# Four-layer graph network kernel: layer 3's bias, relu and residual on other engines, the layer-1 softmax finished in columns, and new piece orders

## The reference

```
x = layernorm(x + (hyperconv2(layernorm(relu(hyperconv1(x)))) + x))                # layer 0
# layer 1, per graph of 64 nodes
w = mask * rowsum(q * (adj @ (k * mask))) / sqrt(256)
x = layernorm(x + softmax(w over the graph's 64 nodes)[:, None] * (x @ Wv))
x = layernorm(x + multi_head_attention(x, scores * 2 adj))                          # layer 2, 8 heads
# layer 3
gate = sigmoid(deg * Wd + bd);  xg = x * gate
QK = sigmoid(xg @ Wqk.T + bqk); S = (QK @ QK.T) / 16 * adj
out = relu((S / (rowsum(S) + 1e-6)) @ xg @ Wl.T + bl + xg @ Wr.T)
x = layernorm(x + out)
```

## Time and profile before

| | |
|---|---|
| three runs | 1066.08, 1060.98, 1060.03 us; median 1060.98 |
| span of the profiled execution, first to last instruction | 1059.4 us; no own total beside the three runs is listed for it |
| median less span | 1.6 us |
| PE busy | 956.5 us, 90% |
| DVE busy | 886.8 us, 84% |
| POOL busy | 777.8 us, 73% |
| ACT busy | 710.6 us, 67% |
| chain that ended last | DVE 33%, PE 25%, issue 14%, ACT 13%, POOL 12% |
| granted PE clock | mean 0.972; 1.00 in all middle stretches |
| DMA queue of the kernel's transfers | 22.2% of 16 engines |

### The profile page before, as it was taken

One profiled execution on the slowest core, in us unless ns is written; L12 is line 12 of the kernel. 1 busy time (PEld: TensorE's weight loads), 2 busy tenths in 40 slices (PEclk: granted clock), 3 DMA queues, 4 the chain that ended last, 5 costly groups with the idle time before them and its releaser, 6 DMA issues.

```text
span 1059.4 us, 32426 instructions
## 1 busy us (share of the span) xinstructions
PE 956.5 (90%) x11164; PEld 808.6 (76%) x11164; DVE 886.8 (84%) x2564; ACT 710.6 (67%) x1516; POOL 777.8 (73%) x1163
## 2 busy tenths in 40 slices
PE   3368999999999999999999999999999999999873
PEld 2256788888888888888888888888888888887752
DVE  4346888898989989989998998989999998989862
ACT  2335677777776677777776677777776777776642
POOL 3155778778877788788877788788877887786542
PEclk9589999999999999999999999999999999999986
DMA  7110221222222122222222112222212112211110
GB/s 206 31 33 9 64 61 53 69 68 59 67 57 61 51 53 57 67 57 67 67 55 62 50 52 60 67 57 67 67 53 62 50 51 62 67 45 42 46 39 20
DMA packets 110231, 61.80 MB, mean 58 GB/s; under 512 B 57072, under 2 KB 105840, under 8 KB 110192
## 3 DMA queue, kind: packets, MB, share of 16 engines
q1 hardware_dynamic: 110192, 61.30, 22.2%
HBM read 35.83 MB, written 8.39 MB: 42 GB/s over the span
## 4 chain that ended last, share of the span: by engine, by line
DVE 33%; PE 25%; issue 14%; ACT 13%; POOL 12%; DMA 1%; DVEq 1%; SPq 0%; POOLq 0%; ACTq 0%
PE bank L460 7%; PE bank L462 6%; PE bank L461 6%; DVE preG L1176 4%; DVE rFl L999 3%; ACT x L735 3%; POOL y0l L1200 3%; ACT r L762 2%; DVE late L1171 2%; PE bank L485 2%; DVE ql L900 2%; PE bank L634 2%; DVE stG L947 2%; DVE PTl L894 2%; DVE xgFl L894 2%
## 5 line engine op out<-in xcount | busy, mean ns | idle before, releaser
L1102 DVE TENSOR_TENSOR late<-bank,acD 128x512 f32<-128x512 f32 x64 | 44.2, 690 | 51.3 <-PE bank L634 50.9
L735 ACT ACTIVATE x<-preB,nbB,rsB 128x256 f32<-128x256 f32 x64 | 35.0, 593 | 68.0 <-POOL nbB L1212 68.0
L460 PE MATMUL bank<-z1h,W 128*128 128x256 f16 x256 | 71.0, 277 | 3.1 <-DVE z1l L894 3.0
L461 PE MATMUL bank<-z1l,W 128*128 128x256 f16 x256 | 70.9, 277 | 0.0
L460 PE MATMUL bank<-W,rFh 128*128 128x256 f16 x256 | 70.8, 277 | 0.0
L462 PE MATMUL bank<-z1h,W 128*128 128x256 f16 x256 | 70.8, 277 | 0.0
L462 PE MATMUL bank<-W,rFl 128*128 128x256 f16 x256 | 70.5, 275 | 0.0
L461 PE MATMUL bank<-W,rFh 128*128 128x256 f16 x256 | 70.5, 275 | 0.0
L1287 POOL TENSOR_TENSOR late<-late,Smx 128x512 f32<-128x512 f32 x64 | 67.0, 1046 | 0.0
L735 ACT ACTIVATE late<-preG,nbG,rsG 128x256 f32<-128x256 f32 x64 | 34.9, 593 | 47.0 <-POOL nbG L1212 46.9
L1200 POOL TENSOR_TENSOR y0l<-y,y0h 128x512 f16<-128x512 f32 x32 | 55.5, 1736 | 1.5 <-ACT y0h L719 1.5
(11 more groups left out here) (284 smaller groups left out, 4625.1 us busy)
## 6 DMA issues: line engine op xcount, KB each, us to landing
Vbd<-vst SPq DMA_DIRECT2D x128, 66.0 KB, 2.1
xin<-x SPq DMA_DIRECT2D x32, 256.0 KB, 2.7
...
Kbd<-kst SPq DMA_DIRECT2D x128, 64.0 KB, 2.0
...
```

The source lines that it names most:

```text
L460: pe.matmul(o, sh, mh, start=start, stop=False, skip_group_check=True)
L461: pe.matmul(o, sh, ml, start=False, stop=False, skip_group_check=True)
L735: m = act.activation(dst[:, t], pre[k][:, t], ACT.Identity, bias=nb[k][:, t:t + 1], scale=rs[k][:, t:t + 1])
L1102: dve.tensor_tensor(Sm[:, t], (bD0, bD1)[t][:].rearrange("p (h k) -> p h k", h=HEADS), acD[:, at.par, t:t + 1].broadcast_to([P, HEADS, NOD ...
```

## The change

Three things change.

1. Layer 3's tail. Before: ACT casts Wr's product out of PSUM into `o2` (scaled), POOL adds the bias `blb` to it, DVE makes `o3` and then `preG` = max(`o3`, 0) + `x3` in one instruction. After: DVE reads Wr's product from PSUM, scales it and adds the bias in one instruction; DVE makes `o3` as before; ACT takes the relu of `o3` into a new tile `o3r`; POOL adds `x3` and writes `preG`.
2. The layer-1 softmax. Before, the differences `wrm` (2 partitions) go through exp, sum, reciprocal and product on 2 partitions, and the product is turned back. After, `wrm` is turned back at once, exp is taken on 128 partitions x 2 columns from PSUM, the sums come from a float32 matmul with a block matrix of ones (`same`), and reciprocal and product are on 128 x 2. DVE loses two pieces, PE gains one, and 1/16 moves into `wpad`.
3. All four order lists are new. In full, PE's:

```diff
-ORDER_PE = [4, 2, 5, 4, 1, 3, 0, 5, 4, 3, 2, 0, 1, 5, 0, 2, 4, 0, 0, 5, 3, 1, 5, 3, 5, 2, 1, 3, 2, 1, 0, 3, 4, 0]
+ORDER_PE = [4, 2, 3, 1, 5, 3, 0, 4, 2, 5, 0, 4, 2, 1, 5, 0, 3, 2, 3, 0, 0, 1, 5, 4, 5, 1, 3, 5, 2, 3, 0, 0, 1, 2, 4]
...
             def stream2(at):
...
-                pe.wait_ge(ev("w_probs"), at.n()).then_inc(ev("pe_held"), 1)
-                pe.transpose(bC[:, 0:TILES], wpr[:].rearrange("t b k -> t (b k)"), ident[0:TILES, 0:TILES]
-                             ).then_inc(ev("p_turned"), 1)
+                pe.wait_ge(ev("w_shifted"), at.n()).then_inc(ev("pe_held"), 1)
+                pe.transpose(bC[:, D:D + TILES], wrm[:].rearrange("t b k -> t (b k)"), ident[0:TILES, 0:TILES]
+                             ).then_inc(ev("w_back"), 1)
+                yield
+                pe.wait_ge(ev("w_exp"), at.n())
+                pe.matmul(bC[:, D + TILES:D + 2 * TILES], same[:], wex[:], start=True, stop=True
+                          ).then_inc(ev("w_sum"), 1)
                 yield
...
-                act.wait_ge(ev("w_shifted"), at.n())
-                act.activation(wex[:], wrm[:], ACT.Exp, scale=SOFT1).then_inc(ev("w_exp"), 1)
+                act.wait_ge(ev("w_back"), at.n())
+                act.activation(wex[:], bC[:, D:D + TILES], ACT.Exp).then_inc(ev("w_exp"), 1)
...
-                act.wait_ge(ev("o2_raw"), at.n())
-                if at.earlier(1):
-                    act.wait_ge(ev("mixed"), at.n(-1))
-                cast(o2[:].rearrange("p t k -> p (t k)"), bG[:], 1.0 / WS).then_inc(ev("o2"), 1)
+                act.wait_ge(ev("mixed"), at.n())
+                if at.earlier(1):
+                    act.wait_ge(ev("preG"), at.n(-1))
+                act.activation(o3r[:], o3[:], ACT.Relu).then_inc(ev("o3_relu"), 1)
...
-                dve.wait_ge(ev("w_exp"), at.n())
-                dve.tensor_reduce(wsm[:], wex[:], AX.X, ALU.add).then_inc(ev("c_softmax"), 1)
-                yield
-                dve.wait_ge(ev("c_softmax"), at.chain(3, 2))
-                dve.reciprocal(wrc[:], wsm[:]).then_inc(ev("c_softmax"), 1)
-                yield
-                dve.wait_ge(ev("c_softmax"), at.chain(3, 3))
-                dve.tensor_tensor(wpr[:], wex[:], wrc[:].rearrange("t (b o) -> t b o", o=1).broadcast_to(
-                    [TILES, 2, NODES]), ALU.mult).then_inc(ev("w_probs"), 1)
-                yield
-                dve.wait_ge(ev("p_turned"), at.n())
-                dve.tensor_scalar(pcol[:], bC[:, 0:TILES], 1.0 / WS, None, ALU.mult).then_inc(ev("p_col"), 1)
+                dve.wait_ge(ev("w_sum"), at.n())
+                dve.reciprocal(wrc[:], bC[:, D + TILES:D + 2 * TILES]).then_inc(ev("c_softmax"), 1)
+                yield
+                dve.wait_ge(ev("c_softmax"), at.chain(2, 2))
+                dve.scalar_tensor_tensor(out=pcol[:], in0=wex[:], scalar=1.0 / WS, in1=wrc[:], op0=ALU.mult,
+                                         op1=ALU.mult).then_inc(ev("p_col"), 1)
...
+                dve.wait_ge(ev("o2_raw"), at.n())
+                dve.scalar_tensor_tensor(out=o2[:], in0=bG[:].rearrange("p (t k) -> p t k", t=TILES), scalar=1.0 / WS,
+                                         in1=blb[:].rearrange("p (o d) -> p o d", o=1).broadcast_to([P, TILES, D]),
+                                         op0=ALU.mult, op1=ALU.add).then_inc(ev("o2"), 1)
+                yield
...
-                dve.wait_ge(ev("mixed"), at.n())
-                dve.scalar_tensor_tensor(out=pre["G"][:].rearrange("p t k -> p (t k)"),
-                                         in0=o3[:].rearrange("p t k -> p (t k)"), scalar=0.0,
-                                         in1=x3[:, at.par].rearrange("p t k -> p (t k)"), op0=ALU.max, op1=ALU.add
-                                         ).then_inc(ev("preG"), 1)
-                yield
...
-                pool.wait_ge(ev("o2"), at.n())
-                bias_tm(o2[:], o2[:], blb).then_inc(ev("o2_biased"), 1)
+                pool.wait_ge(ev("o3_relu"), at.n())
+                if at.earlier(1):
+                    pool.wait_ge(ev("xG"), at.n(-1))
+                pool.tensor_tensor(pre["G"][:], o3r[:], x3[:, at.par], ALU.add).then_inc(ev("preG"), 1)
```

More of the change, by code:

```diff
@@ L184, in build @@
         wpad = sb("wpad", [P, P])
+        same = sb("same", [P, P])
+        wmx = sb("wmx", [TILES, 2])
         wrm = sb("wrm", [TILES, 2, NODES])
-        wmx = sb("wmx", [TILES, 2])
-        wex = sb("wex", [TILES, 2, NODES])
-        wsm = sb("wsm", [TILES, 2])
-        wrc = sb("wrc", [TILES, 2])
-        wpr = sb("wpr", [TILES, 2, NODES])
+        wex = sb("wex", [P, TILES])
+        wrc = sb("wrc", [P, TILES])
         pcol = sb("pcol", [P, TILES])
@@ L218, in build @@
         gt = sb("gt", [P, TILES, D])
+        o3r = sb("o3r", [P, TILES, D])
         g2 = sb("g2", [P, TILES, D])
@@ L906, in _ @@
             dve.memset(onesf[:], 1.0).then_inc(ev("const"), 1)
-            for buf in (atA, aC, atG, wpad):
+            for buf in (atA, aC, atG, wpad, same):
                 dve.memset(buf[:], 0.0).then_inc(ev("const"), 1)
-            dve.wait_ge(ev("const"), 6)
+            dve.wait_ge(ev("const"), 7)
+            for b in range(2):
+                dve.memset(same[64 * b:64 * b + 64, 64 * b:64 * b + 64], 1.0).then_inc(ev("const"), 1)
+            dve.wait_ge(ev("const"), 9)
             dve.wait_ge(ev("ident"), 3).then_inc(ev("cleared"), 1)
@@ L1045, in stream1 @@
                 dve.wait_ge(ev(f"C_in{at.par}"), at.dma(4))
-                dve.tensor_tensor(wpad[:, 0:TILES], wraw[:], mcol[:, at.par], ALU.mult).then_inc(ev("w_masked"), 1)
+                dve.scalar_tensor_tensor(out=wpad[:, 0:TILES], in0=wraw[:], scalar=SOFT1, in1=mcol[:, at.par],
+                                         op0=ALU.mult, op1=ALU.mult).then_inc(ev("w_masked"), 1)
                 yield
@@ L1054, in stream2 @@
                 yield
-                dve.wait_ge(ev("c_softmax"), at.chain(3, 1))
+                dve.wait_ge(ev("c_softmax"), at.chain(2, 1))
                 dve.tensor_tensor(wrm[:], wv, wmx[:].rearrange("t (b o) -> t b o", o=1).broadcast_to(
```

8 lines of the change are left out of this document (4 added, 4 removed).

## The result

The changed kernel takes 1074.31 us (median of 4 runs, 1073.73 to 1074.63) beside 1062.18 for the kernel before (4 runs on the same chip): a ratio of 1.0116, 95% interval 1.0092 to 1.014. It is slower by a little over 1%. I had forecast 1046.5.

The account below looks back on a forecast made before the run. PE's own work plus its waits, mostly on DVE, was taken as the bound: 27.9 + 0.7 + 0.1 + 0.45 + 0.15 = 29.3 us a step. With -15.7 and +1.3 in the drain, 1046.5 us; range 1028 to 1074.

Parts of the forecast that it names:

- Times 27 filled steps: Filled pipeline: 0.58 us less a step than 29.88, over 27 steps, gives -15.7 us.
- wrm's chain: PE ready to turn `wrm`, but DVE makes `Dbg`, `cx`, `Dd`, `wrm` first: 0.7 us a step lost, dearest wait.
- y3l: PE's s3 wants `y3l` at 10.3, after the end of `y3`, a cast and `y3l` itself: 0.1 us lost.
- row sums: PE waits while POOL's `rsq` sums and DVE's `rFl` alternate: 0.3 us lost plus 0.15 for waits, in place of 0.54.
- xg turned: PE's turn of `xg` waits for relu, POOL's added `preG` and `xg` in sequence: 0.15 us lost.
- DVE 25.0: DVE's work a step, 2.2 us less: 25.0 us in place of 27.2.
- Gaps that close: PE's old waits at `wpad`, `xgFl`, `PTl` and `y0l` were to vanish.
- Tail of the last group: In the drain, relu 0.61 and POOL's addition 1.28 with handoffs replace `preG` 0.69: +1.3 us.
- first rival: `HBl` split by POOL's `x2b` in the loop, delaying PE's product: 30.3 us a step, 1073.7 us; chance 0.2.
- Other things that would have shown it wrong: PE waiting on ACT or on the K blocks' DMAs would be wrong in kind; `preG` on POOL expected near 1.28.
- Gain turns into other waits: `pcol` and `Ql` held by POOL on DVE, PE late at layer 3's row sum: 29.8 a step, 1060 us; chance 0.21.
- slack is worth more: Only the `wrm` wait is real on PE: 28.5 us a step, 1025 us; chance 0.15.

Follow-up runs that it names:

- e1: Changed kernel with the old order lists, fitted to the new pieces, in its first six steps; 1067.24 us.
- e10: The kernel of e7 with the old order lists, fitted to the new pieces, in its first six steps; 1037.44 us.
- e11: Changed kernel with one move in DVE's list, `wrm` ahead of `HBl` where it stood behind `Dd`; 1064.62 us.
- e7: Changed kernel with `wrm` ahead of `HBl` and `pcol` behind `stB` on DVE, and `xres`, `xl`, `y0l`, `x2b` as POOL's order; 1056.35 us.
- e2: Changed kernel with `HBl` ahead of `y0` in DVE's list, in all steps; 1101.98 us.
- e3: Changed kernel with `rmm` and `rvar` directly behind `rmean` in DVE's list, in all steps; 1076.63 us.
- e12: The kernel of e7 with `y0l` ahead of `xl` in POOL's list, so POOL waits behind `xres`; 1038.89 us.
- e13: Changed kernel with both the head and the tail of PE's and DVE's lists reordered in the first six steps alone; 1075.05 us.
- e8: Kernel before with only the softmax in columns changed, its old lists fitted to the new pieces; 1079.68 us.
- e16: Kernel before with only layer 3's tail changed, its old lists fitted to the new pieces; 1089.01 us.

## Why the prediction was wrong

**The step that failed** is one that the prediction never took. "Times 27 filled steps" prices the loop, "+1.3" the drain, and the first six steps stand nowhere: they were assumed to be as before. The rows on which the walk rests are all from the full pipeline. The order of the lists was judged by slack that other streams' work provides, and in the fill that work isn't there. This is +17.1 us, more than the whole forecast gain; by e1, 11.8 of it are the lists. Of the other 5.3, about 3 lie in one step that e1 has longer than e10 with the same instructions (the last section), and most of the rest goes with the new code's longer fifth and sixth step.

**The loop's sign was right, its size too large.** Forecast 29.88 to 29.3; measured 29.59.

- *wrm's chain*, 0.7: right in place and kind. PE waits 0.5 to 0.6 at L598, and e11, which removes it, is 0.54 a step faster. It was the dearest wait of the forecast, as stated.
- *y3l*, 0.1, *row sums*, 0.45, and *xg turned*, 0.15: PE or its weight load stands 0.24 (5.8 / 24), 0.33 (8.0 / 24) and 0.25 (5.8 / 23) a step. Together 0.8, forecast 0.7. With 27.9 of PE's own work, 0.5 for `wrm` and 0.36 for `HBl`, of which below, they make up the 29.6.
- *DVE 25.0*: the prices of what goes and comes were right; the two instructions that meet POOL were not in the sum. On PE the new matmul takes 0.14 of slot time for its two halves (L602, mean of 24 steps), priced at 0.13. `HBl` and `pcol` give 2.0 us back (1.4 and 0.65), and 27.1 are measured. `pcol` was seen (0.7) and thought to be covered; that it costs PE nothing was not separated from POOL's list (e7 less e11: 0.35 for both).
- *Gaps that close*: `wpad`, `xgFl`, `PTl` and `y0l` are indeed not in PE's waits.
- *Tail of the last group*: +1.3 forecast, and right. From the start of its `o3` (L1171 before, L1179 after) to its `stG` pass 1.63 us before (1050.77 to 1052.40) and 2.91 after (1062.63 to 1065.54). The two pieces between (timeline):

```profile
1063.54 0.63 ACT L884 ACTIVATE o3r<-late 128x512 f32<-128x512 f32 x1 [4.16 <-DVE late L1179]
1064.25 1.26 POOL L1312 TENSOR_TENSOR preG<-o3r,late 128x512 f32<-128x512 f32 x1 [4.12 <-ACT o3r L884]
```

- *The rest of the drain*, +2.3, was not in the sum. The five intervals between its `stG` marks are 25.6, 22.3, 19.9, 19.2, 19.5 for 24.4, 22.2, 19.4, 18.6, 18.3. The last of them can't be charged to the change: e2, e3, e7 and e10, with the same tail, have 18.3 there too, and others up to 22.1, by the granted clock (the last section). The cause of the others stays open.

**The first rival's mechanism came, in the loop.** `HBl` split by `x2b`, decided by `y0` ending before `xres`: the trace shows just that. The Trainium skill, SBUF — State Buffer, "Who interferes with whom", whose rule that the first to issue goes first I quoted for it, agrees with the trace here: `x2b` issues at 521.60, the second half of `HBl` at 521.71, and `x2b` goes first. The rival should have had more than 0.2. But the rule does not decide every case of this kernel. In the earlier trace rows `y0l` issues 0.11 us ahead of `Ql` too, and there `Ql` goes first, in each of the 24 steps between 200 and 900 us of before (its mean is 0.672 us, and `y0l` takes 1.81). What decides between the two is not shown. The rival's price was wrong: I gave it 1.0 us a step, and the step is 29.6, not 30.3. PE stands 0.36 us (8.2 / 23) for `HBl`, and part of the delay may fall into the `wrm` chain, which starts behind the same product; that is argued, not shown. That the time, 1074.3, is close to the rival's 1073.7 is chance: the rival had the loss in the loop.

**Other things that would have shown it wrong.** The waits view of the loop has no wait of PE on ACT and none on a DMA: right. `preG` on POOL 1.275: right. "Gain turns into other waits" did not decide; "slack is worth more" did not come either: its 28.5 keeps the `wrm` wait and drops the others. e7 and e12 reach 28.7 and 28.2 by taking the waits for `wrm` and `HBl` away, which is another way.

**Open.** What the new lists lose in the fill's steps two to four beyond the head and tail of e13. With old lists and the new code the first `stG` still comes at 176 to 179, not 172.6; the `HT` steps put it on the fifth and sixth (28.5 and 31.6 for 26.9 and 30.0), e8 has 175.9 and e16 177.3, so both parts seem to share in it, argued from one trace each. How much of the fill's loss is the low clock. And the drain's other 2.3 us.
